# Eleven copies of x into the output: issued by ScalarE's queue at the end of stage one, in place of the sync queue along its first half

## The reference, cut to what matters

```python
h = jnp.maximum(_layernorm(x, axis=-1), 0.0)
hh = jnp.einsum('ni,hif->hnf', h, W)
s1 = jnp.einsum('hnf,hf->hn', hh, a1)
s2 = jnp.einsum('hnf,hf->hn', hh, a2)
scores = jax.nn.leaky_relu(s1[:, :, None] + s2[:, None, :], negative_slope=0.2)
scores = jnp.where(adj[None] > 0, scores, -9e15)
att = jax.nn.softmax(scores, axis=-1)
out = jnp.einsum('hnm,hmf->hnf', att, hh)
out = jnp.transpose(out, (1, 0, 2)).reshape(N, 512)
return x + jax.nn.elu(out)
```

## Time and profile before

| | |
|---|---|
| median of 3 runs | 774.72 us (771.73 to 777.65) |
| profiled execution | 777.28 us |
| its span in the trace | 775.6 us |
| mean granted TensorE clock | 0.852 of full |
| busy: PE, DVE, ACT, POOL | 575.2, 651.3, 477.7, 422.4 us |
| bytes moved by DMA | 269.50 MB |

### The profile page before, as it was taken

One profiled execution on the slowest core, in us unless ns is written; L12 is line 12 of the kernel. 1 busy time (PEld: TensorE's weight loads), 2 busy tenths in 40 slices (PEclk: granted clock), 3 DMA queues, 4 the chain that ended last, 5 costly groups with the idle time before them and its releaser, 6 DMA issues.

```text
span 775.6 us, 9118 instructions
## 1 busy us (share of the span) xinstructions
PE 575.2 (74%) x2184; PEld 408.2 (53%) x2184; DVE 651.3 (84%) x1966; ACT 477.7 (62%) x763; POOL 422.4 (54%) x805
## 2 busy tenths in 40 slices
PE   0479798898888788683767868685777659988672
PEld 0245454554444445353556657474656448776561
DVE  4659979899976776775879999999989988999983
ACT  0678977799898989925645666675655223334322
POOL 6634434353333332227766457657756876788850
PEclk9989899999888888875769888877788879999986
DMA  9999999999999999917999999999999887999994
GB/s 287 420 380 388 402 358 382 411 385 419 421 417 391 422 419 419 423 69 229 399 406 417 410 407 398 399 393 407 402 393 354 216 219 176 229 245 281 307 243 157
DMA packets 62395, 269.50 MB, mean 347 GB/s; under 512 B 12050, under 2 KB 12050, under 8 KB 49876
## 3 DMA queue, kind: packets, MB, share of 16 engines
q1 hardware_dynamic: 33520, 185.81, 59.5%
q0 software_dynamic: 25824, 77.31, 32.8%
q10 hardware_dynamic: 2996, 5.77, 2.0%
HBM read 243.49 MB, written 31.13 MB: 354 GB/s over the span
## 4 chain that ended last, share of the span: by engine, by line
DVE 21%; DMA 11%; POOL 10%; issue 8%; ACT 3%; PE 2%; DVEq 0%; ACTq 0%; POOLq 0%
DVE nodes L1156 9%; DMA nodes<-table,list_column 9%; POOL nodes L909 5%; POOL nodes L904 4%; DVE agg L1168 3%; DVE places L274 2%; ACT result L970 2%; DMA nodes<-table,column 2%; ACT result L972 2%; DVE best L263 1%; DVE to_row L1132 1%; DMA out_dram<-result 1%; DVE result L1176 1%; DVE owner L1097 0%; PE psC L1315 0%
## 5 line engine op out<-in xcount | busy, mean ns | idle before, releaser
L698 PE MATMUL psH<-sb_W,normedT 128*128 128x512 f32 x384 | 231.7, 695 | 0.0
L253 ACT ACTIVATE packed<-adj_rows,eight 128x3072 uint8<-128x3072 int32 x66 | 188.7, 2860 | 0.8
L904 POOL DMA_INDIRECT nodes<-table,column x138 | 137.4, 995 | 68.3 <-issue 39.9
L749 POOL TENSOR_TENSOR nodes<-nodes 128x520 f32<-128x520 f32 x47 | 60.9, 1296 | 154.2 <-ACT nodes L663 154.2
L1331 PE MATMUL psP<-nodes,ident 128*128 128x256 f32 x276 | 105.5, 471 | 50.4 <-issue 43.8
L909 POOL DMA_INDIRECT nodes<-table,list_column x109 | 110.1, 1010 | 57.7 <-issue 29.9
L1156 DVE TENSOR_TENSOR nodes<-nodes,psW 128x2048 f32<-128x2048 f32 (+4 forms) x66 | 138.7, 2141 | 0.0
L699 PEld LDWEIGHTS psS<-sb_Wa,normedT 128*128 128x128 f32 x384 | 80.5, 210 | 107.1 <-issue 107.1
L274 DVE FIND_INDEX8 places<-best,packed 128x8 uint32<-128x96 f32 (+6 forms) x240 | 109.9, 466 | 0.0
L263 DVE MAX8 best<-packed 128x8 f32<-128x96 f32 (+6 forms) x240 | 102.7, 459 | 6.4 <-ACT packed L253 6.4
L1332 PE MATMUL psP<-nodes,ident 128*128 128x264 f32 x276 | 102.1, 458 | 0.0
(11 more groups left out here) (182 smaller groups left out, 882.6 us busy)
## 6 DMA issues: line engine op xcount, KB each, us to landing
adj_rows<-in_adj_dram SPq DMA_DIRECT2D x66, 1536.0 KB, 10.2
nodes<-in_adj_dram SPq DMA_DIRECT2D x30, 1536.0 KB, 12.7
table<-nodes SPq DMA_DIRECT2D x48, 260.0 KB, 8.8
sb_x_rows<-in_x_dram SPq DMA_DIRECT2D x48, 256.0 KB, 9.1
out_dram<-in_x_dram SPq DMA_DIRECT2D x11, 512.0 KB, 11.3
result<-in_x_dram POOLq DMA_DIRECT2D x11, 512.0 KB, 7.9
out_dram<-result ACTq DMA_DIRECT2D x11, 512.0 KB, 4.6
out_dram<-result POOLq DMA_DIRECT2D x6, 512.0 KB, 6.5
```

The costliest lines, as they stand in the source:

```text
L253: nc.scalar.activation(words.bitcast(mybir.dt.uint8), sb["adj_rows"][buffer_of(i)][:], ACT.Square, bias=sb["eight"][:], scale=-17.0, accum ...
L698: nc.tensor.matmul(psH[:, t % 2], normedT[:, t % 2, kc], sb["W"][:, kc], start=(kc == 0), stop=(kc == KC - 1))
L904: nc.gpsimd.indirect_dma_start(out=nodes[:, node_at[u] + i * w.direct + j], out_offset=None, in_=table, in_offset=bass.IndirectOffsetOnAxi ...
```

## The change

The eleven copies are the same transfers, from the same rows to the same rows, with the same semaphore. SP no longer issues them. ACT does, all eleven in a row, in its last round (t = 47), behind `turned(47)` and `norm(48)` (which does nothing) and ahead of `h_out(46)` and `h_out(47)`. Each queue works off its DMAs by itself, so the copies now stand in ACT's queue, ahead of the mean row of the table. POOL's wait for `copied` is as before.

```diff
                 for i in range(6, 2 * EARLY + 3):
                     if act_round[occupant(i)] == t:
                         load_adj(sp, sb, adj, i)
-                if t % 2 == 0 and 1 <= t // 2 <= len(COPIED):
-                    copy_nodes(sp, sb, x, out, COPIED[t // 2 - 1])
             sp.wait_ge(h_copied, TILES)
...
             for t in range(TILES):
                 turned(t)
                 norm(t + 1)
+                if t == TILES - 1:
+                    for start in COPIED:
+                        copy_nodes(act, sb, x, out, start)
                 due = [item for item, r in zip(act_items, act_round) if r == t]
```

## The result

| | before | changed |
|---|---|---|
| median of 20 runs each | 774.48 us (768.66 to 779.32) | 779.98 us (775.25 to 788.35) |
| ratio to before, 95% interval | | 1.0071 (1.0049 to 1.0093) |
| profiled execution | 777.28 us | 778.07 us |
| its span | 775.6 us | 776.3 us |

What follows compares the result with a forecast made beforehand. Stage one was taken as bound by ACT's order of work with TensorE's answers, not DMA. Profiled 777.28 + 0 + 0 + 0 + 1.9 = 779.2 us, or 776.6 on the median 774.72; range 769 to 783.

Steps and rivals of the forecast that it cites:

- the signs that I had named: Right: ACT waits near 23 us for PE, mean row releases POOL's first gather; wrong: last `turned` 5 us before 330.
- rival A: Stage one is bound by DMA after all: -13.9 us for the bytes, +1.9 at the seam, 762.7 us; chance 0.06.
- Stage one doesn't wait for the copies: Stage one, 52 to 181 us: taking 5.77 MB off the DMA engines is worth 0, at most 2.0 us.
- my window: 50 to 185 us, where the copies were issued and landed; waits there were to show whether anybody waits for DMA.
- SP's and ACT's issues are free: SP loses eleven issues, ACT gains them before the last two `h_out`, 0.56 us each: worth 0 up to 0.735 each.
- The copies run in the seam: Between stages one and two: copies start at 331.8, take 16.8 us, two stores 0.7 each, engines through at 350.0.
- Who waits for that: POOL's first gather waits for the mean row behind the copies, landing at 350.5 instead of by 348.57: +1.9 us.
- Rival B: Copies alone between the stages run at half pace, 27.5 us; POOL starts 12.6 us too late, 787.3 us; chance 0.08.
- the remainder sum: Copy rate from what loads leave of DMA share in 50 to 175 us: 0.16, or 288 GB/s, 20.0 us.
- The rule that I weighed from the Trainium skill: HBM transfers bound at about 358 GB/s per core; copies counted twice would take 32 us, some 17 us longer.
- Rival C: ACT's queue holds few DMAs, so each copy's issue waits for the one ahead, 1.5 us: 783.4 us; chance 0.03.

Runs made afterwards that it cites:

- before_again: The kernel before, with no edit, profiled a second time: one run, 773.45 us.
- no_copies: The kernel before without the eleven copies and without GpSimd's wait for them: 0.9981 of before (0.9941 to 1.0021).
- pieces_mean_sp: The changed kernel with ten copies in 4 KB pieces, an own buffer for tile 47's rows, and SP storing the mean row: 1.0028 of before.
- act_spread: The changed kernel, but ACT issues the eleven copies in rounds 2 to 22, SP's old places: 1.0008 of before (0.9975 to 1.0041).
- after_again: The changed kernel, with no edit, profiled a second time: one run, 780.04 us.
- sp_last: The kernel before, but SP issues all eleven copies in the last round, on its own queue: 1.0123 of before (1.0077 to 1.0168).
- own_row: The changed kernel with an own buffer for tile 47's rows, so `h_out(47)` needs no store of tile 44: 1.0098 of before (1.0062 to 1.0135).
- five_late: The changed kernel, but ACT issues only the last five copies at the end, SP the other six early: 1.0019 of before (0.9987 to 1.0052).
- own_five: The changed kernel with only five copies late from ACT, six early from SP, and an own buffer for tile 47's rows: 0.9944 of before (0.9901 to 0.9987).
- act_pieces: The changed kernel with ten of the eleven copies in pieces of 4 KB, not 32 KB: 1.0026 of before (0.9996 to 1.0056).

## Why the prediction was right or wrong

The number came inside its range, but that is in part luck: the mechanism was half right and its size wrong by a factor of four, and of the signs that I had named three failed. The last `turned` at 321.2 was my sign of rival A, and it was a false one (before_again). ACT's wait for PE was 12.4 us, not near 23. And POOL's first gather was released by the last store, not by the mean row.

**Stage one doesn't wait for the copies: right in the main.** No ACT wait on a DMA in 50 to 185 us, before or after; no_copies is not distinguishable from before. Rival A (762.7) is out. But my window was too short. Behind it, in 185 to 325 us, VectorE waits for rows of x, whose DMAs stand among the loads. In turn (us in total, times, longest): the first profile of before and pieces_mean_sp (clock 0.84), act_spread and after_again (0.88 and 0.87), before_again and sp_last (0.93); the first of each pair has eleven copies early, the second none.

```profile
DVE stats L562 <- DMA sb_x_rows<-in_x_dram: 6.8, 4, 2.4
DVE stats L567 <- DMA sb_x_rows<-in_x_dram: 0.3, 1, 0.3
DVE stats L560 <- DMA sb_x_rows<-in_x_dram: 19.4, 8, 4.8
DVE stats L560 <- DMA sb_x_rows<-in_x_dram: 9.2, 5, 3.6
DVE stats L562 <- DMA sb_x_rows<-in_x_dram: 15.3, 7, 3.9
DVE stats L563 <- DMA sb_x_rows<-in_x_dram: 10.1, 6, 3.9
```

One of these waits reaches ACT: VectorE's search comes late, and ACT's pack waits for it (`searched`). DVE and then ACT of the changed kernel in order of time:

```profile
287.88 0.70 DVE L560 BATCH_NORM_STATS2 stats<-sb_x_rows 128x6 f32<-128x512 f32 x1 [3.85 <-DMA sb_x_rows<-in_x_dram]
289.55 2.85 ACT L253 ACTIVATE packed<-nodes,eight 128x3072 uint8<-128x3072 int32 x1 [3.26 <-issue]
```

So stage one does touch the DMA limit in its second half, with copies and without. In each pair the wait is longer with them, which speaks for a small gain that I had bounded too low (by the 2.0 us of VectorE in the first half). It is a hint only: over all profiles the wait is 6.8 to 19.4 us with eleven copies early and 0.3 to 16.1 without. Of the profiles, those with eleven copies early have their last `turned` at 330.2, 324.6 and 326.0, the others between 320.8 and 330.4. That stays open.

**SP's and ACT's issues are free: right, with the price off.** ACT paid 7.10/10 = 0.71 us each, not 0.56, just under the 0.735 that I had as the limit. `h_out(46)` came 7.8 us after the last `turned` in place of 5.1, and no wait on the chain ends on it.

**"The copies run in the seam" and "Who waits for that", +1.9 us: the term that was mis-sized.** It measured 8.4 (29.7 against 21.3). That POOL's start waits for the copies' end was named; through what it waits was not, and the sum is out in three places:

- I let the copies start at 331.8 on idle engines, because the profile of before was idle there. But that profile had its last `turned` late. In the seven microseconds after it, the stretch of the first profile of before has DMA share 0.28:

```profile
330.15:337.15 7.00, 7.00 (x24) 3.58 (x23) 6.70 (x25) 1.34 (x4) 1.86 (x2) 0.89 0.28 106
```

The same stretch of before_again has 0.56:

```profile
324.63:331.63 7.00, 7.00 (x21) 3.78 (x20) 6.70 (x30) 1.34 (x4) 1.52 (x2) 0.76 0.56 224
```

That is 2.0 and 3.9 us of leftover loads and stores, which the copies come on top of. The same kernel leaves the DMA engines more or less idle there from one execution to the next, and I had read one.

- I took 16.8 us for the copies, between 14.4 and 20.0. The DMA view of the changed kernel in 319 to 351 us (below: share in 40 slices, and for each queue packets, MB and share) has ACT's queue, q10, at 51.7% of 16 engines, 16.5 us of 32. So the engines' own time was right. But they don't all finish together (the share falls from 0.9 or more to under 0.1 in five slices of 0.8 us), and the elapsed time was 19 (sp_last).

```profile
DMA  9998999897989699889394969565311000000036
...
q10 hardware_dynamic: 354, 5.77, 51.7%
q1 hardware_dynamic: 736, 2.49, 19.7%
```

- I gave the last two stores 0.7 us each. They took 16.6 and 9.4 us from issue to landing, and landed with or behind the last copy (25.1 and 25.8 us after the last `turned`, the copy 24.9). I had asked only for the mean row, and had it behind all the copies. It wasn't: issued at 343.09, its one packet of 2080 bytes moved at 343.8 and its semaphore was full at 344.2, ahead of the last copy at 346.1. The sentence of the Trainium skill that the prediction quotes (page "DMA: Bandwidth & Descriptors", section "Queues, rings and completion order") has descriptors consumed in ring order on one engine; that the mean row stays behind all the copies doesn't follow from it, and the trace disagrees. The store of tile 47, on the other queue, was what POOL waited for (347.0).

The medians differ by 5.5 us, the seams by 8.4. Behind the seam all profiles take the same within 2.7 us, so the other 3 us most likely come back in stage one; no_copies' interval allows it. No run settles it.

**What I didn't see: `h_out(47)` waits for the store of tile 44.** The wait is in the code (`stored[t % HB]`) and in the order (`table_stored2`). I wrote that `h_out(47)` can't start before PE is done, and didn't ask what else it waits for. With eleven copies it made no difference to the end (own_row); with five it made all of it (five_late against own_five). Nor could I see in the landings, which tell only of the last step, that fifteen sixteenths of that store had long arrived. Why one sixteenth lags, and already does by 1.8 us in the kernel before, no run shows.

**Rival B** (half pace, 27.5 us of copying, +12.6): not so; 19 us. But its direction was right, and the 288 GB/s of the remainder sum, which I averaged away, was nearer to the 304 measured than 400 was. The rule that I weighed from the Trainium skill (page "DMA: Bandwidth & Descriptors", section "Where 436 GB/s comes from") would have had 32 us, the prediction's estimate with a copy counted twice: the trace disagrees by 13. The same page's section "Queues, rings and completion order" says that an engine drains a packet of some 9 to 17 descriptors from one queue before it turns to the next. act_pieces agrees in kind: what a turn of the other queue costs hangs on the size of its pieces. The count of 9 to 17 no run here shows.

**Rival C** (each issue waits for the one ahead): not so, 0.71 us an issue against 1.5.

## What to carry to other kernels

Before transfers are moved into a gap, ask which completions are due in that gap, on every queue: they may land only when the moved transfers are through, whenever they were issued, and a small store beside large pieces on another queue can wait for its last part alone. Then move as many as the slack of the first due completion holds, not all: five of eleven here, and only once tile 47 had its own buffer. And when a wait is found in the chain, look for what runs beside it; own_row took 7 us out of the chain for nothing, and the same edit was worth 6 us of seam once the other limit had been eased.

## What the runs showed that I had not expected

- Copies from DRAM to DRAM, eleven in a row, move with the store behind them 315 GB/s at DMA share 0.97 (sp_last), against 416 to 420 for loads of adj at 1.01 and 1.02.
- A store of 260 KB lands in 2.0 us on idle engines. The last four of the changed kernel and of own_row, beside eleven copies in 32 KB pieces on the other queue, take 9.4 to 24.9 us (24.9 is own_row's store of tile 45, issued at 324.8); act_pieces' last four, beside pieces of 4 KB, take 8.3 to 15.0.
- Fifteen sixteenths of a store can be there 11.7 us before the last one, and ACT waits for that last one (`h_out(47)` of the changed kernel).
- The same kernel reaches the same point of its program 5.5 us apart in two executions, with the granted clock at 0.84 and 0.93 in 185 to 325 us, while the stretch behind it repeats within 0.2 us (two profiles of each kernel).
